# Eleven weight loads moved from ScalarE's instruction stream to SyncE's in the last head of an attention kernel

## The reference, cut to what matters

```python
h = _layernorm(x) * (1 + ca) + sa
x = x + ga * attention(h)           # 8 heads x 2 batches: 16 turns of the phase below
h = _layernorm(x) * (1 + cb) + sb
for l in range(2):                  # local layers; the loads that move are layer 0's
    qkv = shift_token(h) @ wqkv[l]; q, k = rotary_xpos(l2norm(q) * qs, l2norm(k) * ksc)
    h = h + local_attention(q, k, v) @ wo[l]
    h = h + feed_forward(h)
```

## Time and profile before

| what | value |
|---|---|
| median of 3 runs | 2799.52 us (2797.24 to 2800.05) |
| the profiled execution, its own time | 2807.97 us |
| its span in the profile | 2806.3 us |
| PE busy, share of the span | 2569.5 us, 92% |
| DVE busy | 2177.3 us, 78% |
| ACT busy | 1558.0 us, 56% |
| POOL busy | 544.0 us, 19% |
| mean granted TensorE clock, share of full speed | 0.954 |

### The profile page before, as it was taken

One profiled execution on the slowest core, in us unless ns is written; L12 is line 12 of the kernel. 1 busy time (PEld: TensorE's weight loads), 2 busy tenths in 40 slices (PEclk: granted clock), 3 DMA queues, 4 the chain that ended last, 5 costly groups with the idle time before them and its releaser, 6 DMA issues. The chain is left out here.

```text
span 2806.3 us, 45372 instructions
## 1 busy us (share of the span) xinstructions
PE 2569.5 (92%) x14104; PEld 1551.7 (55%) x14104; DVE 2177.3 (78%) x4594; ACT 1558.0 (56%) x3447; POOL 544.0 (19%) x388
## 2 busy tenths in 40 slices
PE   4995999999999999986999999979979999997998
PEld 1442433333333333324677777668857777775877
DVE  4776999999999999975788888645558888885665
ACT  0221566667666667652566666633436666665442
POOL 0110011111111010105333333200023333331000
PEclk7997899999999999988999999989989999999999
DMA  2334355445454445444100000030020000001121
GB/s 88 114 114 114 87 139 141 116 111 128 113 135 137 121 107 129 115 149 127 66 17 21 16 16 21 16 127 17 12 59 8 9 9 8 9 12 47 45 66 39
DMA packets 124307, 205.19 MB, mean 73 GB/s; under 512 B 22704, under 2 KB 71408, under 8 KB 120800
## 3 DMA queue, kind: packets, MB, share of 16 engines
q1 hardware_dynamic: 109440, 164.23, 21.4%
q0 software_dynamic: 8832, 21.80, 2.7%
q10 hardware_dynamic: 5920, 17.75, 1.7%
HBM read 125.57 MB, written 54.26 MB: 64 GB/s over the span
## 5 line engine op out<-in xcount | busy, mean ns | idle before, releaser
L949 PE MATMUL o_ps<-probs,vx 128*33 128x512 f32 (+3 forms) x2560 | 549.0, 551 | 10.7 <-ACT probs L1004 10.7
L1002 ACT ACTIVATE probs<-st_ps 128x512 f32<-128x512 f32 (+3 forms) x640 | 339.0, 530 | 334.5 <-PE st_ps L934 183.7
L1060 DVE SCALAR_TENSOR_TENSOR geo_x<-geo_rows,kp_t 128x512 f32<-128x512 f32 (+3 forms) x640 | 439.5, 710 | 14.5 <-ACT probs L1004 14.5
L1039 DVE TENSOR_REDUCE chunk_max<-a_ps 128x1 f32<-128x512 f32 (+3 forms) x640 | 359.0, 603 | 42.1 <-PE a_ps L917 36.9
L1004 ACT ACTIVATE probs<-geo_x 128x512 f32<-128x512 f32 (+3 forms) x640 | 360.8, 564 | 12.9 <-DVE geo_x L1066 12.8
L1309 PE MATMUL local_in_ps<-w_local,local_ht 128*128 128x512 f32 x1152 | 324.5, 419 | 9.4 <-ACT local_sq L1451 5.2
L1470 ACT ACTIVATE local_probs<-local_s_ps,local_bias,local_inv 128x256 f32<-128x256 f32 x512 | 282.6, 563 | 13.8 <-DVE local_bias L1565 13.8
L917 PE MATMUL a_ps<-k,q 96*128 96x512 f32 (+3 forms) x640 | 239.7, 449 | 43.6 <-DVE chunk_max L1039 36.2
L1748 PE MATMUL ff_ag_ps<-ff_ht_parts,w 128*128 128x512 f32 (+1 forms) x1056 | 257.8, 402 | 19.5 <-DVE ff_gate L1857 11.3
L949 PEld LDWEIGHTS o_ps<-probs,vx 128*33 128x33 f32 x2560 | 124.4, 112 | 272.7 <-issue 185.1
L1477 ACT ACTIVATE local_pt<-local_pt_ps 128x512 f32<-128x512 f32 x256 | 152.3, 596 | 209.3 <-PE local_pt_ps L1367 201.1
(11 more groups left out here) (175 smaller groups left out, 3833.8 us busy)
## 6 DMA issues: line engine op xcount, KB each, us to landing
geo_rows<-geo SPq DMA_DIRECT2D x64, 512.0 KB, 7.6
q<-q_parts SPq DMA_DIRECT2D x48, 256.0 KB, 4.2
k<-k_parts SPq DMA_DIRECT2D x48, 256.0 KB, 6.4
piece_lo<-in_pieces POOLq DMA_DIRECT2D x15, 768.0 KB, 6.0
weight_parts<-piece_hi SPq DMA_DIRECT2D x15, 768.0 KB, 3.4
weight_parts<-piece_lo SPq DMA_DIRECT2D x15, 768.0 KB, 6.0
raw<-out_t SPq DMA_DIRECT2D x128, 64.0 KB
shares_in<-shares SPq DMA_DIRECT2D x64, 128.0 KB, 4.9
```

What stands on the lines that cost most here:

```text
L949: ins = pe.matmul(o_ps[kind * HALF:kind * HALF + VW, g % 2, off:GTOK], vx[s][:, j, :], probs[:, i % PSLOTS, kind, off:GTOK], start=j == 0, ...
L1002: act.activation(probs[:, s % PSLOTS, 0, off:GTOK], st_ps[:, (b * NB + s) % STBANKS, off:GTOK], ACT.Exp).then_inc(q["st_used"], 1)
L1039: dve.reduce_max(chunk_max[:, it, c:c + 1], a_ps[:, n % ABANKS, 0:width], AX.X).then_inc(q["a_used"], 1)
L1060: ins = dve.scalar_tensor_tensor(out[:, off:GTOK], geo[:, 1, at], kp_t[:, j, ds(b, 1)].rearrange("p o -> p o"), geo[:, 0, at], ALU.add, AL ...
```

## The change

The function `load_local` is cut in three (`load_inputs` for the two DMAs of `w_local`, `load_tables` for the eight of tables and scales, `load_output` for `wo_local`) and still calls all three for layer 1. For layer 0 ScalarE's block goes, and SP gets the two waits and the eleven DMAs in its last turn: the first two behind `maxima_in(b, 1)` and ahead of `send(b, 0, s)`, the other nine behind `send(b, 0, s)` and ahead of `maxima_in(b, 2)`.

```diff
@@ SP's turn
                 maxima_in(b, 1)
+                if not more:
+
+                    sp.wait_ge(q["values_in"], BH + START)
+                    sp.wait_ge(q["pv_done"], b * NB + PV0 + START)
+                    W.load_inputs(sp, S, 0)
                 send(b, 0, s)
+                if not more:
+                    W.load_tables(sp, S, io, 0)
+                    W.load_output(sp, S, io, 0)
                 maxima_in(b, 2)
@@ ScalarE's turn
-                    if not more and s == 4:
-
-                        act.wait_ge(q["values_in"], BH + START)
-                        act.wait_ge(q["pv_done"], b * NB + PV0 + START)
-                        W.load_local(act, S, io, 0)
@@ LayerWeights
     def load_local(self, eng, S, io, layer):
+        self.load_inputs(eng, S, layer)
+        self.load_tables(eng, S, io, layer)
+        self.load_output(eng, S, io, layer)
+
+    def load_inputs(self, eng, S, layer):
         first, q = layer * PER_LAYER, S.local
         for part in range(2):
             eng.dma_start(self.w[:, part, :, :].bitcast(F32), S.pieces[part, ds(first + WQKV_PIECE, CC)].rearrange("k p n -> p k n")).then_inc(q["w"], 16)
+
+    def load_tables(self, eng, S, io, layer):
+        q = S.local
         for k in range(4):
             eng.dma_start(self.table[:, k, :, :].rearrange("p t d -> p (t d)"), io["xpos"][k]).then_inc(q["tables"], 16)
             eng.dma_start(self.scale[:, k, :], io["qk_scale"][ds(layer, 1), k, :].to_broadcast([P, LD])).then_inc(q["tables"], 16)
+
+    def load_output(self, eng, S, io, layer):
+        first, q = layer * PER_LAYER, S.local
         eng.dma_start(self.wo[:, :, :].rearrange("p k n -> p (k n)"), io["pieces"][ds(first + WO_PIECE, 1), :, 0:KIN * C].rearrange("o p n -> p (o n)")).then_inc(q["wo"], 16)
```

## The result

| measurement | before, median | changed, median | ratio, 95% interval | gain |
|---|---|---|---|---|
| first | 2799.78 us | 2783.29 us | 0.9942 (0.9925 to 0.9959) | 16.2 us (11.5 to 21.0) |
| second | 2810.09 us | 2794.11 us | 0.9931 (0.9910 to 0.9953) | 19.4 us (13.2 to 25.3) |
| third | 2808.73 us | 2792.54 us | 0.9947 (0.9926 to 0.9969) | 14.9 us (8.7 to 20.8) |

A gain is one minus the ratio, times the median before. The change makes the kernel faster, by more than was predicted: 2783.29 us lies 1.5 us under the low end of the range, 2784.8. The 12.41 us of the prediction lie in the interval of the first and third measurement, not in the second's. The three gains together, weighted by the widths of their intervals, give an estimate of 16.7 us (13.6 to 19.9), which leaves 12.41 out.

What follows compares the result with a forecast made beforehand. TensorE and VectorE bound the attention phase, and ScalarE's eleven load issues in head 15 stopped both. Removing 12.41 us and adding 0 gave 2787.1 us, range 2784.8 to 2794.3.

Steps and rivals of the forecast that it cites:

- The sum: Whole kernel: 12.41 us removed, 0 added, handed on whole after head 15, giving 2787.1 us, 0.44% faster.
- What is removed: Head 15, TensorE from the maxima ahead of step 6 to step 12's scores: 21.83 against head 14's 9.42, 12.41 us removed.
- What is added on SP: Head 15, SP: eleven issues, held until about 4.85 MB are through at 1220.9, covered by 3.7 us of idle time.
- The transfers in one queue: Head 15, SP's queue: part 2 of the maxima lands 0.4 to 2.8 us before step 24's scores need it; no wait.
- rival 1: Head 15, step 24: part 2 of the maxima lands late, TensorE waits 2.1 us; gain 7.3 us, 2792.2; chance 0.18.
- The users of the weights: After head 15's loads: users of the weights come late enough; layer 1's loads stay unchanged, their issues taking 10.16 us.
- Rival 2: Head 15, ScalarE: without the profiler the hold is shorter, at least 5.4 us; gain 5.3 us, time 2794.2; chance 0.12.

Runs made afterwards that it cites:

- the run with the copies: Changed kernel plus eleven DRAM-to-DRAM copies of the same sizes as the loads, issued by ScalarE in the setup phase: ratio 0.9947 (0.9932 to 0.9961).

## Why the prediction was wrong

The mechanism in head 15 and its place were right. The sum was too small by a term that it put at nothing, layer 1's issues (3.4 us), and by a removed term read from one execution (1.0 us too low as a mean).

1. **What is removed.** Right in mechanism. The stretch went from 21.83 to 9.41 us, the 12.4 us as forecast. It was read from one execution, and is too low as a mean: the two other traces with the hold have 23.32 and 23.33 us, so it is 12.4 to 13.9 us, with a mean of (21.83 + 23.32 + 23.33)/3 - 9.41 = 13.4 us. The 1.5 us between the traces are the lower clock, which in those two still held for eight products of step 6 and 7 (2.79 us at 1232.04 in the second trace).
2. **What is added on SP.** Right that nothing is paid, and too careful in size: SP was free 11.4 us after the piece's second store, not 13.6. Its longest issue took 1.81 us, so ScalarE's 5.60 us did not go with the loads. The reading of these long issues as a queue that takes no more until some bytes are done isn't shown, and the amount taken from ScalarE's queue didn't carry over: the eleventh issue passed when some 4.2 MB had moved since 1203, not 4.85. Layer 1's issues speak against bytes alone, since with the same bytes ahead of them they took 7.6 us or 10.
3. **The transfers in one queue.** Right in what came of it: the queue was full until about 1224.5, part 2 was issued behind it and came in time. The issue was 3.7 us later than forecast, because POOL's store of the maxima took 3.2 to 3.7 us longer to land with the DMA engines full, a term that the sum didn't have. It cost nothing only because the time from issue to use, 1225.44 - 1222.50 = 2.9 us, was enough. There was hardly any room: in the run with the copies the same load was 0.62 us late, which is rival 1 at a small size. That one queue keeps its order, on which rival 1 rested, is borne out by the run with all loads ahead of part 1, where the wait of 12.57 us is. The Trainium skill (DMA: Bandwidth & Descriptors, Queues, rings and completion order) says that on each DMA engine descriptors are consumed in ring order, and that run agrees with it. I hadn't seen that two queues do worse: with the large loads on ScalarE's queue part 1 was 2.07 us late, while the prediction saw it only as a small gain for part 1.
4. **The users of the weights** holds the step that failed: "Layer 1's loads are left as they are; there the eleven issues take 1846.93 + 1.52 - 1838.29 = 10.16 us". I took the issue time of an instruction as its own, to be left out of the sum because the instruction isn't changed. The runs showed 7.6 to 7.7 us there, TensorE's wait behind them shortened from 3.3 and 2.4 us to between 0.8 and 1.1 us, and the feed forward from 228.95 us (mean of 229.9 and 228.0) to 225.6 us (mean of 225.0, 226.0 and 225.8), 3.4 us less.
5. **The sum.** 13.4 + 3.4 = 16.8 us, where the three measurements have 16.2, 19.4 and 14.9. A mean of medians and of single traces agrees that well partly by chance.
6. **The rivals and the range.** No rival came true in the three traces of the changed kernel. Rival 2, a hold shorter without the profiler, pulled the range the wrong way: nothing in the time of the runs speaks for it. The low end of the range had only the spread of three runs under it, 1.4 us to each side, and no case for a gain that the row didn't show. That spread was far too narrow: the 29 runs of the kernel before in the second measurement lie between 2803.36 and 2817.57 us. So it is in part luck on which side of 2784.8 a median of four runs fell; that something was missing is shown by the second measurement and by the traces.

Still open: why the queue's past changes an issue's length. The patterns repeat within 0.3 us in different executions and on different chips, so it is no noise; what in the past sets it, no run here tells. The copies carried the same 5.9 MB as the loads that they stand for, and brought back 1.8 of the 2.4 us. It is open too why ScalarE's queue held one issue for 5.60 and 5.91 us in head 15, and SP's none over 1.81 with the same bytes in the changed kernel. And the 3.4 us of the feed forward are shown in traces, not by a ratio of runs.

## What to carry to other kernels

An engine at 56% can be the bound where it issues DMAs: add up the issues in its stream, and look at the longest of them, not at the count. The cost is the stop of the engines behind it plus the time at the lower clock after it. When loads are moved to another queue, ask for each small transfer that a step waits for what will stand ahead of it on its own queue and what will share the DMA engines with it from the others; here two large loads on a second queue made a small one on the first late in step 4, and did no harm in step 12. The stores that such a load waits for get slower too while the DMA engines are full. And look at every other place that issues on the queue that was relieved, for it may change too.

## What the hardware showed unexpectedly

The time of an issue depends on what its queue carried long before: eleven equal issues took 7.6 to 7.8 us in four traces with nothing of layer 0 on ScalarE's queue, 9.46 us with copies on it some 1,800 us earlier, and 10.0 to 10.8 us with layer 0's loads, all or a part, on it. A wait of 2.07 us for a load cost 5.4 us of head 15, since the products behind it ran at the lower clock (3.63 us for eight instead of 1.91). A store of 4 KB landed 1.5 us after its issue with the DMA engines nearly empty, and 4.7 to 5.6 us after it with another queue's loads filling them. The Trainium skill (DMA: Bandwidth & Descriptors, Issuing engines are not separate DMA queues) says that issuing from several engines saves only issue time; these runs agree for the bytes: 345 GB/s before, 346 changed and 340 with the two large loads on ScalarE, while the queues were full. The issue time was not small beside them: one issue took 5.60 us, and the stop that it made cost TensorE 12.4 us.
